# A four-part transformer kernel on one core: three pieces of work moved in the order of its engines, and a second buffer for routing weights

## The reference

```python
x = x + _L0_xattn_ref(_layernorm(x), ctx_1024, ...)   # attention, one head of 256, then gelu(out @ W1 + b1) @ W2 + b2
x = x + _L0_ffn_ref(_layernorm(x), ...)               # 8 experts, top 2, swiglu
x = x + _L1_xattn_ref(_layernorm(x), ctx_1024, ctx_1024, mask_BxSxS2_bk1, ...)   # 16 heads of 64
x = x + _L1_ffn_ref(_layernorm(x), ...)               # 64 experts of 64, top 8, and 2 shared of 512
```

## Time and profile before

| What | Value |
|---|---|
| time, three runs | 1584.42 us median, 1583.55 to 1587.38 |
| the profiled execution | 1585.53 us |
| its span, first to last instruction | 1583.8 us |
| mean granted TensorE clock | 0.981 of full |
| busy share of PE, DVE, ACT, POOL | 94%, 65%, 44%, 20% |
| HBM, over the span | 72 GB/s |

### The profile page before, as it was taken

One profiled execution on the slowest core, in us unless ns is written; L12 is line 12 of the kernel. 1 busy time (PEld: TensorE's weight loads), 2 busy tenths in 40 slices (PEclk: granted clock), 3 DMA queues, 4 the chain that ended last, 5 costly groups with the idle time before them and its releaser, 6 DMA issues.

```text
span 1583.8 us, 24931 instructions
## 1 busy us (share of the span) xinstructions
PE 1495.1 (94%) x8762; PEld 1171.7 (74%) x8762; DVE 1027.2 (65%) x2446; ACT 702.6 (44%) x1512; POOL 320.8 (20%) x347
## 2 busy tenths in 40 slices
PE   5998999997999888999999999998999899999998
PEld 4888887884566565566566666666888799999997
DVE  7767654564657668766666677675565676767654
ACT  2323322333655465666666666674352222232321
POOL 2202001243243415000000000021212333333321
PEclk8999999998999999999999999999999999999999
DMA  8432020312454110100000000001003755455341
GB/s 273 162 105 96 9 63 23 138 71 83 163 171 137 54 29 27 35 12 1 14 21 18 12 1 28 1 1 32 28 4 97 153 120 120 122 119 125 89 102 59
DMA packets 78180, 115.54 MB, mean 73 GB/s; under 512 B 7447, under 2 KB 51813, under 8 KB 77797
## 3 DMA queue, kind: packets, MB, share of 16 engines
q1 hardware_dynamic: 74981, 105.50, 23.7%
q0 software_dynamic: 3072, 8.39, 1.7%
HBM read 95.00 MB, written 18.87 MB: 72 GB/s over the span
## 4 chain that ended last, share of the span: by engine, by line
PE 55%; DVE 4%; issue 3%; ACT 2%; DMA 1%; POOL 0%; SPq 0%; DVEq 0%; ACTq 0%; POOLq 0%
PE PS L67 12%; PE PS L68 11%; PE PS L69 11%; PE PS L2536 7%; PE PS L2548 6%; PE PS L2524 5%; PE PS L2563 3%; ACT c_pr L2632 1%; DMA d_wb<-wscratch 1%; DVE c_sm L2741 0%; DVE c_pr L2750 0%; DVE c_c L2716 0%; PE PS L1845 0%; DVE X L1072 0%; DVE d_h L890 0%
## 5 line engine op out<-in xcount | busy, mean ns | idle before, releaser
L1918 ACT ACTIVATE d_hf<-PS,C 128x512 f32<-128x512 f32 x160 | 108.5, 690 | 268.7 <-PE PS L69 255.7
L2641 ACT ACTIVATE c_pt<-PS 100x512 f32<-100x512 f32 x256 | 138.9, 595 | 142.0 <-PE PS L2536 141.8
L67 PE MATMUL PS<-d_w,d_h 128*128 128x256 f32 x640 | 186.1, 291 | 12.2 <-DVE X L1990 10.8
L885 POOL CAST d_h<-d_hf 128x512 fp32r<-128x512 f32 x160 | 128.3, 815 | 312.5 <-DVE d_hf L2000 246.6
L68 PE MATMUL PS<-d_w,d_h 128*128 128x256 f32 x640 | 183.5, 287 | 0.0
L69 PE MATMUL PS<-d_w,d_h 128*128 128x256 f32 x640 | 183.4, 287 | 0.0
L2632 ACT ACTIVATE c_pr<-c_sm,c_mn 128x400 f32<-128x400 f32 x256 | 158.4, 626 | 28.2 <-DVE c_mn L2741 28.2
L2741 DVE CUSTOM_DVE_ANT_0 c_sm<-PS,c_mw 128x400 f32<-128x400 f32 x256 | 136.1, 569 | 26.3 <-PE PS L2524 21.6
L2536 PE MATMUL PS<-ident,c_pr 128*100 128x128 f32 x1024 | 139.2, 279 | 0.0
L890 DVE TENSOR_TENSOR d_h<-d_hf,d_h 128x512 fp32r<-128x512 f32 x160 | 129.4, 865 | 12.9 <-POOL d_h L885 12.9
L67 PEld LDWEIGHTS PS<-d_w,d_h 128*128 128x128 f32 x640 | 125.1, 196 | 15.5 <-issue 13.7
(11 more groups left out here) (301 smaller groups left out, 3033.8 us busy)
## 6 DMA issues: line engine op xcount, KB each, us to landing
d_wb<-wscratch SPq DMA_DIRECT2D x64, 512.0 KB, 7.8
a_cT<-ctxT SPq DMA_DIRECT2D x4, 1601.0 KB, 7.7
a_nat<-ctx SPq DMA_DIRECT2D x4, 1536.0 KB
zs<-e_zero SPq DMA_DIRECT2D x2, 2944.0 KB, 18.1
ys<-e_y SPq DMA_DIRECT2D x46, 128.0 KB, 1.7
e_z<-zs SPq DMA_DIRECT2D x10, 512.0 KB, 4.1
d_w1r<-l_w SPq DMA_DIRECT2D x10, 512.0 KB, 4.4
d_w2r<-l_w SPq DMA_DIRECT2D x10, 512.0 KB, 6.2
```

The lines of the kernel that those rows point to most:

```text
L67: pe.matmul(out, w[0], x[0], start=first, stop=False)
L885: i = eng.tensor_copy(mem["h"][b % 2][0][:, m, :], mem["hf"][:, m, :])
L1918: act.activation(memD["hf"][:, m, :], PS[:, m, :], ACT.Silu, bias=C[:, b1 + g * 4 + m:b1 + g * 4 + m + 1]).then_inc(DM["act"], 1)
L2641: act.activation(c_pt[u % 2][0:KW, h, :, i * P:(i + 1) * P], PS[0:KW, BT + h, :].rearrange("p (t q) -> p t q", q=P), ACT.Copy).then_inc(F[ ...
```

## The change

Six edits, in three places.

1. First stage, DVE: `shift(1)` and the low part of the value weights stand at the end of tile 0, ahead of the mask flags, and no longer ahead of its copies.
2. First stage, POOL and SP: the first half of the dense weights is split after `ln_scale(2)` (it waited for `ln_scale(1)`), the second half after the power of batch 3. SP loads the second half after the loads of batch 1.
3. Dense stage: for batch 1 `logits` and `turn_logits` stand one tick earlier, `count(0)`, `places(0)` and `blocks_table(0)` two. ACT makes batch 1's logits after one of unit 6's four activations. DVE spreads the last two low parts of unit 6 between the plan's steps.
4. The casts of unit 7 go from POOL to ACT, and POOL issues scatters 0 to 5, the power of batch 2, then 6 to 15.
5. Last stage: `d_w` has two halves; DVE's third and fourth use wait for the transposes of the first and second.
6. SP loads the routing weights of each batch right behind its store, and the weights of group 3 behind the second store.

```diff
--- before.py
+++ after.py
@@ -225,7 +225,7 @@
         d_nm = sb("d_nm", [P, NT])
         d_sm = sb("d_sm", [P, NT])
         d_rsm = sb("d_rsm", [P, NT])
-        d_w = sb("d_w", [P, QT, E1])
+        d_w = sb("d_w", [P, 2, QT, E1])
         d_wT = [sb(f"d_wT{b}", [E1 + ES, 512]) for b in range(B)]
         d_b2 = sb("d_b2", [E1 + ES, D])
         stD.close()
@@ -465,7 +465,6 @@
             load_mask(0)
             m_sync(sp, 0)
             load_turned(1)
-            m_sync(sp, 1)
             sp.wait_ge(A["pad"], 3)
             for g in range(GR):
                 sp.dma_start(zs[g].rearrange("(n p) d -> p n d", p=P),
@@ -475,6 +474,8 @@
                     load_turned(b + 1)
                 load_mask(b)
                 load_plain(b)
+                if b == 1:
+                    m_sync(sp, 1)
 
         def q_banks(b):
 
@@ -683,12 +684,12 @@
             pool.tensor_copy(a_bk[:, :, :], C[:, COLS["bk"][0]:COLS["bk"][0] + KD].unsqueeze(2).to_broadcast([P, KD, P])
                              ).then_inc(A["pad"], 1)
             ln_rstd(pool, 0, [1])
-            pool.wait_ge(LN["z"], 2 * QT)
+            ln_rstd(pool, 0, [2])
+            pool.wait_ge(LN["z"], 3 * QT)
             split_all(pool, M, memM, 0, 0)
-            ln_rstd(pool, 0, [2])
+            ln_rstd(pool, 0, [3])
             split_all(pool, M, memM, 1, 1)
             tables(pool)
-            ln_rstd(pool, 0, [3])
 
         def a_dve(dve):
             def product():
@@ -772,10 +773,6 @@
                 if n == 0:
                     dve.wait_ge(A["csum"], QT + 1)
                     ln_scale(dve, 0, 1)
-                    shift(1)
-                    dve.wait_ge(A["w_hi"], 2)
-                    dve.tensor_tensor(a_w[1][:, 1, :, :], a_raw[:, 2, :, :], a_w[0][:, 1, :, :].bitcast(F32),
-                                      ALU.subtract).then_inc(A["w_lo"], 1)
                 if i == QT - 1 and b + 1 < B:
                     for k in range(KD):
                         context(b + 1, k)
@@ -803,6 +800,11 @@
                     if i == 1:
                         queries_back(b + 1)
 
+                if n == 0:
+                    shift(1)
+                    dve.wait_ge(A["w_hi"], 2)
+                    dve.tensor_tensor(a_w[1][:, 1, :, :], a_raw[:, 2, :, :], a_w[0][:, 1, :, :].bitcast(F32),
+                                      ALU.subtract).then_inc(A["w_lo"], 1)
                 dve.wait_ge(flag_in, b * 16 + 16)
                 dve.tensor_reduce(fl_a[:, n:n + 1], fl_m[:, i, 0:W0], AX.X, ALU.min).then_inc(flag_red, 1)
                 dve.tensor_reduce(fl_b[:, n:n + 1], fl_m[:, i, W0:S2], AX.X, ALU.min).then_inc(flag_red, 1)
@@ -1184,15 +1186,15 @@
                         turns(b, [0])
                     if at == 22:
                         turns(b, [1])
-                    if at == 25:
+                    if at == 25 - b:
                         logits(b)
-                    if at == 27:
+                    if at == 27 - b:
                         turn_logits(b)
+                if t == 44:
+                    count(0)
                 if t == 46:
-                    count(0)
+                    places(0)
                 if t == 48:
-                    places(0)
-                if t == 50:
                     blocks_table(0)
                 if t == 60:
                     pe.wait_ge(SP_["planned"], PLAN[0] + PL)
@@ -1385,10 +1387,15 @@
                 m_gelu(act, 2 * b + 3)
                 high(b)
                 z_add(b)
-                m_gelu(act, 2 * b + 4, (0, 1))
+                m_gelu(act, 2 * b + 4, (0, 1) if b == 0 else (0,))
                 logits_out(b)
-                m_gelu(act, 2 * b + 4, (2, 3))
-            m_gelu(act, 7)
+                m_gelu(act, 2 * b + 4, (2, 3) if b == 0 else (1, 2, 3))
+            act.wait_ge(M["h_hi"], 7 * 4)
+            for m in range(4):
+                m_gelu(act, 7, (m,))
+                if m:
+                    high_hidden(act, M, memM, 7, 7, m - 1, 4, M["act"])
+            high_hidden(act, M, memM, 7, 7, 3, 4, M["act"])
             prefill(0)
             prefill(1)
             high(2)
@@ -1455,16 +1462,9 @@
                 both_rstd(b)
                 high(2 * b + 3, (2, 3))
                 high(2 * b + 4)
-            scatter(pool, 0, ALL[0:2])
-            high(7, (0,))
-            scatter(pool, 0, ALL[2:3])
-            high(7, (1,))
+            scatter(pool, 0, ALL[0:6])
             both_rstd(2)
-            scatter(pool, 0, ALL[3:4])
-            high(7, (2,))
-            scatter(pool, 0, ALL[4:5])
-            high(7, (3,))
-            scatter(pool, 0, ALL[5:])
+            scatter(pool, 0, ALL[6:])
             both_rstd(3)
             scatter(pool, 1, ALL)
             for q in range(0, 24):
@@ -1724,12 +1724,14 @@
                 two_greatest(b)
                 their_places(b)
                 ownership(b)
-                if b == 1:
-                    running_counts(0)
-                low(2 * b + 4, (2, 3))
+                if b == 0:
+                    low(4, (2, 3))
+            running_counts(0)
             block_counts(0)
+            low(6, (2,))
             slots(0)
             owners(0)
+            low(6, (3,))
             m_add(2)
             moments(2)
             table(0)
@@ -1796,17 +1798,14 @@
             for b in range(B):
                 sp.wait_ge(DR["wt_out"], (B + b) + 1)
                 sp.dma_start(wscratch[0:E1, b * S:(b + 1) * S], d_wT[b][0:E1, :]).then_inc(DR[f"stored{b % 2}"], 16)
-                if b < 2:
-                    sp.wait_ge(DR[f"stored{b % 2}"], 16)
-                    by_token(GS, b, b)
-            for g in range(GS, GD):
+                if b == 1:
+                    weights(GS + 1)
+                sp.wait_ge(DR[f"stored{b % 2}"], 16 * (b // 2 + 1))
+                by_token(GS, b, b)
+            for g in range(GS + 1, GD):
                 if g + 1 < GD:
                     weights(g + 1)
                 for b in range(B):
-                    if g == GS and b < 2:
-                        continue
-                    if g == GS:
-                        sp.wait_ge(DR[f"stored{b % 2}"], 32)
                     by_token(g, b, (g - GS) * B + b)
 
 
@@ -1870,7 +1869,7 @@
                 pe.wait_ge(DR["lt_out"], 2 * B)
                 wait_past(pe, DR["wt_out"], B + b if b else 0)
                 for i in range(QT):
-                    last = pe.transpose(PS[0:E1, 6, i * P:(i + 1) * P], d_w[:, i, :], ident[:, :])
+                    last = pe.transpose(PS[0:E1, 6, i * P:(i + 1) * P], d_w[:, b % 2, i, :], ident[:, :])
                 last.then_inc(DR["wt"], 1)
 
             hidden(0)
@@ -1974,13 +1973,13 @@
                 dve.wait_ge(DR["own"], own + 2 * QT + 2)
                 dve.reciprocal(d_rts[:, ts], d_ts[:, ts]).then_inc(DR["own"], 1)
                 dve.wait_ge(DR["own"], own + 3 * QT + 3)
-                wait_past(dve, DR["wt"], B + b if b else 0)
-                dve.scalar_tensor_tensor(d_w[:, :, :], d_mr[:, :, :], -1.0, d_pr[:, ts, :], ALU.is_equal,
+                wait_past(dve, DR["wt"], B + b - 1 if b >= 2 else 0)
+                dve.scalar_tensor_tensor(d_w[:, b % 2, :, :], d_mr[:, :, :], -1.0, d_pr[:, ts, :], ALU.is_equal,
                                          ALU.mult).then_inc(DR["sel"], 1)
                 dve.wait_ge(DR["sel"], b + 1)
                 for i in range(QT):
                     n = b * QT + i
-                    dve.tensor_scalar(d_w[:, i, :], d_w[:, i, :], d_rts[:, n:n + 1], None, ALU.mult).then_inc(DR["w"], 1)
+                    dve.tensor_scalar(d_w[:, b % 2, i, :], d_w[:, b % 2, i, :], d_rts[:, n:n + 1], None, ALU.mult).then_inc(DR["w"], 1)
 
             def add_second(u):
                 b = u % B
```

## The result

The changed kernel takes **1569.3 us** (median of 4 runs, 1567.52 to 1569.79), the kernel before 1584.12 us beside it (1583.55 to 1587.38): ratio 0.990, interval 0.9883 to 0.9917. The forecast was 1568 us within 1556 to 1577, "faster" with 0.94.

A forecast was written before the change was run, and what follows sets the result against it. TensorE, busy for 94% of the span, was taken as the bound, leaving its idle and low-clock time to win. +6.0 - 5.2 - 17.3 = -16.5 us gave a median of 1568 us, range 1556 to 1577.

The forecast's parts named there:

- Tile 0: First stage: TensorE's 6.83 us gap before tile 0's last transpose group goes, -6.8 us.
- I leave the clock here at 0: Tile 0: no gain or loss from TensorE's clock, 0 us, between -2 and +1.
- First split: End of tile 2: POOL's split slows `shift(2)`, +5.5 us before tile 3's transposes; the gap lowers the clock, +2.2.
- Second split and adds: Tiles 6 and 7: tile 6's bias waits less, -0.4 us; bias adds slow `ln_scale(3)`, delaying tile 7, +5.5.
- Whole first stage: First stage, sum of -6.8, -0.4, +5.5, +2.2 and +5.5: +6.0 us.
- Plan: End of dense stage: earlier plan steps and fewer POOL casts start the last scatter and experts earlier, -5.2 us.
- The casts' -2.8: Scatters: four casts leave POOL's chain, 2.8 us; six scatters in DVE's densest stretch cost at most 1.3 us.
- Last stage: Last stage: five units at steady pace take 57.1 us of 74.43, -17.3; -8.7 if third gap and low clock stay.
- Number 1: First stage: POOL's moved work meets nothing; 5.5, 2.2 and 5.5 fall away, -29.7, 1555 us; chance 0.17.
- Number 2: Last stage: routing weights still arrive late and the last gap stays; -8.6 for the stage, 1576 to 1577 us; chance 0.15.
- 3: Dense stage's end: the plan's move gives nothing, another wait holding the first expert blocks; 1573 us; chance 0.03.
- 4: First stage: TensorE's clock stays at 1.2 GHz from tile 3's gap until tile 7; +16.5, 1601 us; chance 0.03.

The follow-up runs named there:

- first_only: Kernel before with only the first stage's edits (SyncE's loads, POOL, DVE): 1619.64 against 1617.13 us, ratio 1.002.
- shift_move: Changed kernel with POOL's splits and SP's loads of the first stage as in the kernel before: 1558.04 us, ratio 0.9851 to the kernel before.
- last_sp: Kernel before with only the routing-weight loads right behind each store, and one `d_w`: ratio 0.9963.
- last_only: Kernel before with only the last stage's edits (two halves of `d_w`, routing-weight loads behind each store): 1601.0 us, ratio 0.9893.
- paced: Changed kernel, POOL's splits released behind the context's low halves, each bias add by DVE's reciprocal of tiles 8 to 11: 1551.95 us, ratio 0.9804.
- ctx_late: Changed kernel with both POOL splits released behind the context's low halves in tiles 3 and 7: 1593.25 us, ratio 0.9859 to the kernel before.
- both_late: Changed kernel with both POOL splits released by the last instruction of `shift(2)` and `shift(3)`: 1594.48 us, ratio 0.9865 to the kernel before.
- after_again: The changed kernel run again, unaltered, on another chip: 1596.54 against 1615.94 us for the kernel before, ratio 0.9881.

## Why the prediction held, term by term

The total was right to 1.3 us, and not all by its terms: the first stage was forecast 4.0 us too dear and the plan 2.2 too good, and 1.95 us of lower clock came in where nothing was changed.

- **Tile 0, -6.8, clock 0.** The gap went exactly, and `shift(1)` beside tile 1's maximum cost nothing, as `first_only` and `shift_move` show. The attend came 8.4 us earlier, 1.6 more than the gap: after one gap instead of two the clock stood at 0.77 from 29.2 to 36.71 us; before it was 0.50 from 29.2 to 42.6 us. The step that failed is "I leave the clock here at 0": a gap that goes can take its share of the slow time with it. -2 was my bound. How much it takes is not the same in every execution. Besides its second gap, tile 0 took 8.4 to 10.5 us from the first transposes to the attend in the seven traces with this stage as before (10.1 in mine), and 8.4 in the changed kernel.
- **First split, +5.5 and +2.2.** From the attend of tile 0 to that of tile 3 the kernel lost 6.1 us (8.4 ahead, then 2.3). Tile 2 gave 0.5 of its own (its gap of 0.36 us went), so tile 3 alone cost 6.6. The price of `shift(2)` was right, 5.4 us. Behind the new gap, from the transposes to the attend, tile 3 took 9.14 us instead of 7.93, though its old gap of 1.62 us ahead of the last transpose shrank to 0.32: the lower clock cost 2.5 us, near my 2.2. The term that I had left out is this old gap, -1.3, which the new one covers. It stands in the trace of the kernel before:

```profile
81.27 0.30 PE L585 MATMUL PS<-ident,a_p 128*65 128x128 f32 x1 [1.62 <-DVE a_pt L795]
```

- **Second split and adds, -0.4 and +5.5.** Lost 4.4 us between the attends of tiles 4 and 7 (99.37 to 149.35 against 101.67 to 147.29): -0.4 at tile 6, as forecast, and +4.7 at tile 7. The scaling took 6.3 us more (priced at 5.5, bound 6.9), but the 1.49 us that tile 7 waited for its copies before were within the new gap: 0.33 was left.
- **Whole first stage, +6.0.** +2.0 by the traces, 0 to +7 by `first_only`. The size of this term also depends on which execution of the kernel before it is set against. In the seven profiles that hold its first stage unchanged, the attend of tile 8 stands at 157.65 to 163.77 us, median 161.5; in the three that hold the changed one at 164.8 to 165.2. Against the median the stage costs 3.4 us. The spread has two parts. One is the clock in tiles 0 and 7. The other is the gap of tile 0 itself, 4.33 to 6.95 us in these seven. In `last_sp`, which has the smallest, POOL's first cast waited longer for its load and began 1.30 us after the first instruction of `shift(1)`, in my trace 0.39 us; three of the four custom instructions were through in their 0.42 us instead of one. TensorE in `last_sp`:

```profile
34.79 0.45 PE L585 MATMUL PS<-ident,a_p 128*65 128x128 f32 x1 [4.33 <-DVE a_pt L795]
```

- **Plan, -5.2.** -3.0. First scatter -1.9 instead of -2.4. The casts' -2.8 was the step that failed: I set six scatters in DVE's densest stretch at 1.3 us at most, and one alone took 1.8 us more than its 0.97. The estimate that the Trainium skill ("SBUF — State Buffer", section "SBUF: two separate sides") led to, -3.9, was nearer: by it a GpSimd DMA cannot write its descriptors while DVE runs an instruction in a two-port mode. The long scatter stands beside DVE's two-tile products and two low halves and ends 0.8 us after them in all eight traces, which fits that DVE holds it up. Whether these instructions run in such a mode no trace shows. The rule should have weighed more than a mean over scatters that had other neighbours. That the neighbours cause it was not tried by itself.
- **Last stage, -17.3.** -16.9, shown alone by `last_only`, and by halves. The split into 8.7 and 8.6 came out as 10.8 and 8.3 with an overlap of 2.2.
- **Rivals.** Number 1 (POOL's work meets nothing, 0.17) fell; `paced` is what it would have been, and more. Number 2 (weights late, 0.15), 3 and 4 fell: after the new gap of tile 3 the granted clock stood at 1.00 again from 83.75 to 99.37 us, the next tile.

## What to carry to other kernels

When a long GpSimd instruction moves, the question is not which engine waits for its result but which DVE instructions stand beside it: read from a trace what each DVE instruction takes its inputs from, and release POOL's work so that only readers of TensorE's banks and reductions are beside it. Even an instruction of one column counts, if the exponential waits for it. And when two edits sit in one change, a mark on the bounding engine behind each of them prices them singly, where whole times differ by less than the chip does.

## What had not been expected of the hardware

**A blocked DVE instruction can be held by more than one POOL instruction.** In the changed kernel one DVE instruction passed for each of POOL's. In `ctx_late` a single one of 128x1 took 9.27 us, the length of all four adds behind one another, though its record begins 0.02 us ahead of the first. The Trainium skill ("SBUF — State Buffer", section "Who interferes with whom") has the one that issues first hold the ports for one instruction. That DVE has to wait agrees; that it waits for four does not follow from it. The same section lets a DVE instruction with at most one input in SBUF pass, outside its two-port modes: the maxima (1.82 us) and the copies (0.69 us) from the banks bear that out.

**POOL is slowed as well.** Its subtraction of 128x1024 took 2.36 us beside nothing sensitive, 2.52 beside the shift, and in `both_late` 3.92 beside the context's low halves, though the subtraction ahead of it took 2.35 beside them.

**Chips differ most in the experts' stretch.** From the first `e_z` to the first scores of the cross attention the kernels took 172.2 to 175.0 us on two chips and 199.4 to 206.4 on those of the first two sets, whatever the kernel. `after_again` has TensorE idle there, with nothing that the trace shows it to wait for:

```profile
442.22 0.47 PE L1211 MATMUL PS<-ident,e_z 128*128 128x128 f32 x1 [6.44 <-issue]
```

A second such gap, of 6.12 us, stands at 500.78. What lies behind them was not tried. `ctx_late` was 6.2 us ahead of `after_again` at `e_z` and took 2.4 us longer for this stretch (202.45 against 200.06), so that only part of its lead reached the end.
